# Attention over 32 sequences on one core: reciprocals of softmax sums formed on Pool, and gates from tanh

## The reference

```python
scores = jnp.einsum('bhqd,bhkd->bhqk', q, k) / jnp.sqrt(dk)      # layer 2: 16 heads of 8; layer 3: 16 heads of 64
attn = jax.nn.softmax(scores, axis=-1)
ctx = jnp.einsum('bhqk,bhkd->bhqd', attn, v)
...
# layer 2, slots (64 per batch entry), a GRU step on the routed inputs gi
r = jax.nn.sigmoid(xr + hr)
z = jax.nn.sigmoid(xz + hz)
n = jnp.tanh(xn + r * hn)
h_new = (1.0 - z) * n + z * hs
```

## Time and profile before

| what | value |
|---|---|
| time before, median of 3 runs | 2606.22 us (2602.77 to 2616.06) |
| time of the profiled execution | 2609.04 us |
| its span, first to last instruction | 2607.1 us |
| busy: PE, DVE, ACT, POOL | 78%, 59%, 51%, 24% of the span |
| mean granted TensorE clock | 0.872 of full speed |

### The profile page before, as it was taken

The page is one execution under the profiler, slowest core; times in us unless marked ns, Lnnn a source line. Parts: engine busy times, 40 slices in busy tenths (PEclk is TensorE's granted clock), DMA queues, the critical chain, the costliest instruction groups (busy, mean ns, idle before and its releaser), DMA issues.

```text
span 2607.1 us, 50762 instructions
## 1 busy us (share of the span) xinstructions
PE 2029.3 (78%) x17664; PEld 1624.5 (62%) x17666; DVE 1539.7 (59%) x4062; ACT 1316.8 (51%) x4486; POOL 629.4 (24%) x628
## 2 busy tenths in 40 slices
PE   3878888878788887345778888888888888788864
PEld 2667776767677765134556566666767666666654
DVE  5877676666576677633445565655556555554442
ACT  1755554545455655323456666555555555444411
POOL 0011112121211120012233342242332423222321
PEclk9789898899899988556589999998898989999987
DMA  7024443343444410300000011121212212222243
GB/s 227 26 77 123 125 135 92 121 128 106 117 140 124 131 53 1 129 30 20 12 9 12 5 53 57 57 72 57 72 59 64 60 58 72 59 87 70 80 141 100
DMA packets 149515, 205.94 MB, mean 79 GB/s; under 512 B 11088, under 2 KB 105360, under 8 KB 149008
## 3 DMA queue, kind: packets, MB, share of 16 engines
q1 hardware_dynamic: 141072, 185.90, 24.2%
q0 software_dynamic: 8192, 16.79, 2.1%
HBM read 162.80 MB, written 39.85 MB: 78 GB/s over the span
## 4 chain that ended last, share of the span: by engine, by line
PE 33%; DVE 9%; ACT 7%; issue 6%; POOL 1%; DMA 0%; DVEq 0%; ACTq 0%; SPq 0%; POOLq 0%
PE ps L1529 5%; PE ps L1752 5%; ACT pb L1915 4%; PE ps L1731 3%; DVE nm L2260 3%; PE ps L1562 3%; PE ps L1738 2%; ACT pt L1923 2%; PE ps L1589 2%; PE ps L1778 2%; PE ps L1571 2%; PE ps L1555 2%; DVE hT L2054 1%; PE ps L1770 1%; DVE hT L2049 1%
## 5 line engine op out<-in xcount | busy, mean ns | idle before, releaser
L1915 ACT ACTIVATE pb<-ps,nm 128x128 f32<-128x128 f32 x1024 | 363.2, 378 | 285.3 <-DVE nm L2260 276.3
L1956 POOL TENSOR_TENSOR pb<-pb,rcs 128x512 f32<-128x512 f32 x256 | 267.6, 1046 | 896.8 <-DVE rcs L2250 894.7
L936 ACT ACTIVATE pb<-pb,nm 128x128 f32<-128x128 f32 x1024 | 313.0, 392 | 88.1 <-DVE nm L1147 86.2
L2260 DVE TENSOR_REDUCE nm<-ps 128x8 f32<-128x1024 f32 x128 | 156.1, 1220 | 180.8 <-PE ps L1731 108.5
L1752 PE MATMUL ps<-w,pb 128*128 128x128 f32 x1024 | 177.6, 302 | 96.1 <-ACT pt L1923 74.1
L1915 ACT ACTIVATION_READ_ACCUMULATOR pb<-ps,nm 128x1 f32 x1024 | 223.0, 218 | 0.0
L2269 DVE COPY pt<-ps 128x512 f32<-128x512 f32 x128 | 88.3, 690 | 210.4 <-PE ps L1752 210.4
L1529 PE MATMUL ps<-hT,big 128*128 128x128 f32 x960 | 153.9, 310 | 72.7 <-DVE hT L2054 66.0
L1752 PEld LDWEIGHTS ps<-w,pb 128*128 128x128 f32 x1024 | 128.4, 155 | 129.1 <-issue 89.9
L1529 PEld LDWEIGHTS ps<-hT,big 128*128 128x128 f32 x960 | 135.3, 216 | 100.1 <-DVE hT L2054 79.9
L828 PE MATMUL ps<-w,pb 128*128 128x128 f32 x1024 | 160.0, 302 | 18.5 <-ACT pb L936 15.2
(11 more groups left out here) (355 smaller groups left out, 4457.2 us busy)
## 6 DMA issues: line engine op xcount, KB each, us to landing
big<-in_we SPq DMA_DIRECT2D x120, 514.0 KB
big<-in_we SPq DMA_DIRECT2D x120, 384.0 KB
big<-sorted_in SPq DMA_DIRECT2D x16, 960.0 KB
sorted_out<-big SPq DMA_DIRECT2D x32, 256.0 KB
sorted_in<-big SPq DMA_DIRECT2D x8, 960.0 KB, 9.0
hidden<-h_all SPq DMA_DIRECT2D x8, 512.0 KB, 2.9
h_all<-hidden SPq DMA_DIRECT2D x8, 512.0 KB, 3.9
sorted_out<-h_all SPq DMA_DIRECT2D x16, 256.0 KB
```

What stands on the lines that cost most here:

```text
L936: m = a.activation(pb[:, n % 2, k * S:(k + 1) * S], pb[:, n % 2, k * S:(k + 1) * S], ACT.Exp, bias=nm[:, n % 2, k:k + 1])
L1915: m = a.activation(pb[:, n % 2, e * S:(e + 1) * S], ps[:, half, k * S:(k + 1) * S], ACT.Exp, bias=nm[:, n % 2, e:e + 1], accum_out=sums[:, ...
L1956: g_.tensor_tensor(p4, p4, r4.unsqueeze(2).to_broadcast([P, 4, S]), ALU.mult).then_inc(n2["p_normed"], 1)
L2260: v.tensor_reduce(nm[:, n % 2, :], ps[:, 0:2, :].rearrange("p a (j k) -> p (a j) k", k=S), AX, ALU.max, negate=True).then_inc(n2["maxed"], 1)
```

## The change

The reciprocals of the sums leave DVE. In `norm`, POOL now waits for the exponentials itself, raises the four sums to the power -1 (a TENSOR_TENSOR with the new tile `minus`, 128 x 4), waits for that, and multiplies. `sums_inv` is gone from DVE's list, and so is its wait for `p_normed` two units before. The sigmoid of the gates is replaced by tanh(x/2): with t = tanh(x/2), sigmoid(x) is (t + 1)/2. The factor 1/2 of the first gate goes into `hn_c` in the setup (one more DVE instruction, once). The products with the gates become `scalar_tensor_tensor` with + 1 inside, and the factor 1/2 of the second gate goes into the last addition. The counts of instructions of the slots stay.

```diff
--- before.py
+++ after.py
@@ -129,6 +129,7 @@
         identb = sb("identb", [P, P], BF16)
         ones = sb("ones", [P, P])
         half = sb("half", [P, G])
+        minus = sb("minus", [P, 4])
         sc = sb("sc", [P, 16])
         hmax = sb("hmax", [P, NG * NC1])
         ymax = sb("ymax", [P, NG])
@@ -465,6 +466,7 @@
             def _(g):
                 g.memset(ones[:, :], 1.0)
                 g.memset(half[:, :], -0.5)
+                g.memset(minus[:, :], -1.0)
                 g.memset(hmax[:, :], 0.0)
                 g.memset(va[:, :, :, :], 0.0).then_inc(setup_g, 1)
                 g.wait_ge(setup_g, 1)
@@ -520,7 +522,8 @@
                 v.tensor_tensor(c1[0:HR, :], ps[0:HR, 3, 0:1], W("b1s", HR), ALU.add)
                 link(v.tensor_tensor(crz[:, :], ps[:, 4, 0:2 * D], R("bhh")[:, 0:2 * D], ALU.add))
                 v.tensor_tensor(crz[:, :], crz[:, :], R("bih")[:, 0:2 * D], ALU.add)
-                v.tensor_tensor(hn_c[:, :], ps[:, 4, 2 * D:3 * D], R("bhh")[:, 2 * D:3 * D], ALU.add)
+                link(v.tensor_tensor(hn_c[:, :], ps[:, 4, 2 * D:3 * D], R("bhh")[:, 2 * D:3 * D], ALU.add))
+                v.tensor_scalar(hn_c[:, :], hn_c[:, :], 0.5, None, ALU.mult)
 
             @block.tensor
             def _(pe):
@@ -1869,7 +1872,7 @@
                     g = group_at(hs, 22)
                     if g is not None and place == 2:
                         a.wait_ge(slot["rz_in"], g + 1)
-                        a.activation(rz, rz, ACT.Sigmoid).then_inc(slot["rz"], 1)
+                        a.activation(rz, rz, ACT.Tanh, scale=0.5).then_inc(slot["rz"], 1)
                     g = group_at(hs, 23)
                     if g is not None and place == 1:
                         a.wait_ge(slot["n_in"], g + 1)
@@ -1950,9 +1953,12 @@
                     g_.tensor_tensor(x_group(g), x_group(g), row_bcast(bias, G), ALU.add).then_inc(n2["bias_" + bias], 1)
 
                 def norm(n, half):
+                    g_.wait_ge(n2["exps"], 2 * n + half + 1)
+                    p4 = pb[:, n % 2, 4 * half * S:4 * (half + 1) * S].rearrange("p (k s) -> p k s", k=4)
+                    at = 8 * (n % 2) + 4 * half
+                    r4 = rcs[:, at:at + 4]
+                    g_.tensor_tensor(r4, sums[:, at:at + 4], minus[:, :], ALU.pow).then_inc(n2["sums_turned"], 1)
                     g_.wait_ge(n2["sums_turned"], 2 * n + half + 1)
-                    p4 = pb[:, n % 2, 4 * half * S:4 * (half + 1) * S].rearrange("p (k s) -> p k s", k=4)
-                    r4 = rcs[:, 8 * (n % 2) + 4 * half:8 * (n % 2) + 4 * half + 4]
                     g_.tensor_tensor(p4, p4, r4.unsqueeze(2).to_broadcast([P, 4, S]), ALU.mult).then_inc(n2["p_normed"], 1)
 
                 for hs in range(FIRST, LAST + 1):
@@ -2193,14 +2199,14 @@
                     if g is not None and place == 1:
                         v.wait_ge(slot["rz"], g + 1)
                         v.wait_ge(slot["xn_in"], g + 1)
-                        slink(v.tensor_tensor(rz[:, :, 0:D], rz[:, :, 0:D], hn_c[:, :].unsqueeze(1).to_broadcast(both),
-                                              ALU.mult))
+                        slink(v.scalar_tensor_tensor(rz[:, :, 0:D], rz[:, :, 0:D], 1.0,
+                                                     hn_c[:, :].unsqueeze(1).to_broadcast(both), ALU.add, ALU.mult))
                         v.tensor_tensor(xn, xn, rz[:, :, 0:D], ALU.add).then_inc(slot["n_in"], 1)
                     if g is not None and place == 2:
                         v.wait_ge(slot["n"], g + 1)
                         slink(v.tensor_tensor(hnew, hs_rows(), xn, ALU.subtract))
-                        slink(v.tensor_tensor(hnew, hnew, rz[:, :, D:2 * D], ALU.mult))
-                        v.tensor_tensor(hnew, hnew, xn, ALU.add).then_inc(slot["new"], 1)
+                        slink(v.scalar_tensor_tensor(hnew, rz[:, :, D:2 * D], 1.0, hnew, ALU.add, ALU.mult))
+                        v.scalar_tensor_tensor(hnew, hnew, 0.5, xn, ALU.mult, ALU.add).then_inc(slot["new"], 1)
                     g = group_at(hs, 24)
                     if g is not None and place == 2:
                         v.wait_ge(slot["val_psum"], g + 1)
@@ -2242,17 +2248,8 @@
                 def hs_rows():
                     return hs_c[:, :].unsqueeze(1).to_broadcast(both)
 
-                def sums_inv(n, half):
-                    at = 8 * (n % 2) + 4 * half
-                    v.wait_ge(n2["exps"], 2 * n + half + 1)
-                    if n >= 2:
-                        v.wait_ge(n2["p_normed"], 2 * (n - 2) + half + 1)
-                    v.reciprocal(rcs[:, at:at + 4], sums[:, at:at + 4]).then_inc(n2["sums_turned"], 1)
-
                 for hs in range(FIRST, LAST + 1):
                     n, p = unit_at.get(hs), unit_at.get(hs - 1)
-                    if p is not None:
-                        sums_inv(p, 1)
                     if n is not None:
                         v.wait_ge(n2["scores"], n + 1)
                         if n >= 2:
@@ -2260,8 +2257,6 @@
                         v.tensor_reduce(nm[:, n % 2, :], ps[:, 0:2, :].rearrange("p a (j k) -> p (a j) k", k=S), AX, ALU.max,
                                         negate=True).then_inc(n2["maxed"], 1)
                     work(1, hs)
-                    if n is not None:
-                        sums_inv(n, 0)
                     if p is not None:
                         v.wait_ge(n2["transposed"], 2 * p + 2)
                         if p >= 2:
```

## The result

The changed kernel takes 2633.64 us (median of 4 runs, 2629.57 to 2648.62) against 2606.33 us for the kernel before: a ratio of 1.011, 95% interval 1.0077 to 1.0143. It is slower, by more than the 0.5% that the measurement can tell, and outside my range of 2598 to 2628.

The account below looks back on a forecast made before the run. PE was busiest, 78% of 2607.1 us, with delays between engines costing full length in lone units. Terms +11.0 (way), -1.3 (DVE), -1.5 and -1.9 (gates) gave +6.3 us, so 2612.5 us, range 2598 to 2628.

Parts of the forecast that it names:

- The longer way (part 1): From exponentials to product on POOL, power and self-wait replace DVE's reciprocal and hop: 11.0 us slower, paid mainly in lone units.
- The first lone stage: Start of the second half, 1133 to 1315 us, where units do not overlap others: forecast 6 to 8 us longer.
- In the other units ... There the price is nothing: In at most 116 other units, every half is ready before PE transposes it, so the later product costs nothing.
- some 14 us lost to the products before: Estimate for the kernel before: DVE instructions lengthened by overlap with POOL's 256 wide products, some 14 us in all.
- rival 2: POOL's powers hold up DVE as its products do: 14 us lost again, half showing, 2620 us; chance 0.07 beyond +13.
- The sign that I had named: The forecast would be wrong if, among other signs, DVE's L2110 or L338 became longer.
- What DVE gets back: Of DVE's 43.9 us of reciprocals, only those directly ahead of something urgent count: 1.3 us faster.
- Part 2: Tanh for sigmoid at the gates: 16 table loads go, exponentials start 0.74 us earlier; 1.5 and 1.9 us gained.
- number 1: POOL becomes late more widely: all 32 lone units pay 1.1 us, 2636 us, half-way 2620 to 2628; chance 0.15 beyond +13.

Follow-up runs that it names:

- e4: Kernel before, plus an unused power on POOL ahead of its wait for DVE's reciprocal, which the product still uses: ratio 1.0030, again 1.0047.
- e2: Kernel before with the reciprocals as a power on POOL, the sigmoid left: ratio 1.0061, again 1.0083 and 1.0093.
- e9: Kernel before, plus one extra power of 128 x 4 on POOL behind each product, nobody waiting for it: ratio 1.0012.
- e5: No reciprocals on DVE or POOL; POOL multiplies by the sums directly behind the exponentials (results are no attention): ratio 1.0080 to the kernel before.
- e8: Kernel before, plus one extra product of constants, 128 x 384, on POOL behind each product, nobody waiting for it: ratio 1.0138.
- before_again: The kernel before, unchanged, run once more for a second profile: ratio 0.9977.

## Why the prediction was wrong

**The longer way (part 1): right.** Power 1.02 and self-wait 0.08 us forecast, 1.03 and 0.08 measured. The first lone stage 6 to 8 us longer forecast, 5.8, 6.1 and 4.9 in three profiles. The whole way 11.0 us forecast, 8 to 12 measured by e4, which has it nearly alone.

**"In the other units ... There the price is nothing": this step failed.** It asked whether each half of the probabilities is ready before PE transposes it. It is; but the product's place beside DVE moved, and that has a price of its own: held time rose from 16.4 to 48.7 us. The 25 to 27 us of it that e2 has above e4 went with 0.31 and 0.36%, 8 to 9 us, on two chips, and this is net of what DVE got back. I had the row in hand, `qm` up to 1309 ns beside wide work on POOL, and my estimate of some 14 us lost to the products before was near the 16.4. But I priced from it what powers might do (rival 2) and not what products would do when released earlier. The sign that I had named, a longer L2110, does not even show it (337 ns in the mean before, 340 after); the held time came in lines that the reciprocal had kept clear, the layer norms' L330 above all. The power is harmless (e9), and the product is not (e5, e8). The Trainium skill (GPSIMD Engine Reference, Key points) names contention in SBUF between GpSimd and those VectorE instructions that are in a two-port mode or have two SBUF inputs. The runs show it as 0.17 us becoming 1.00 for a wide product, and nothing for a power of four elements; which instructions are in a two-port mode no run here shows.

**"What DVE gets back": half of it.** I forecast -1.3 us and saw the reciprocals as cost only. In the trace DVE is 5.0 us busier without them. No run has the 1.3 us by themselves. The reciprocals' other effect, to hold the product back until DVE turned to PSUM, stood in no row by itself but in the order of rows: 223 of the 256 products start within 0.1 us of a reciprocal's end.

**Part 2: the mechanism right, its size off.** The 16 loads went. The timeline at the gate of the earlier trace rows, in the kernel after:

```profile
1385.46 1.22 DVE L2257 TENSOR_REDUCE nm<-ps 128x8 f32<-128x1024 f32 x1
1385.58 0.63 ACT L1875 ACTIVATE h_all<-h_all 128x512 f32<-128x512 f32 x1 [2.37 <-DVE h_all L2195]
...
1386.71 0.37 ACT L1918 ACTIVATE pb<-ps,nm 128x128 f32<-128x128 f32 x1 [0.50 <-DVE nm L2257]
```

The exponentials are 0.03 us behind the maxima where they had been 0.78 behind. Forecast -3.4 us; alone it measured 0.28 to 0.49%, 7 to 12 us (4 to 12 by the medians), and beside a late product none was seen.

**The sum.** Forecast: 11.0 for the way, -1.3 for DVE, -3.4 for the gates, +6.3 in all. Measured: 8 to 12 for the way, 8 to 9 for the held time less what DVE got back, nothing seen for the gates, 16 to 21 in all, against 20.7 to 27.3 from the three ratios of the whole (0.79 to 1.10%). The rest is within the intervals and is not assigned. Of the rivals none was it: number 1 gives a time near this one, but by waits that did not become wide (34 in place of 24, not all 64 halves of the lone units), and e5 is slower with hardly any way to pay.

The version to keep is e1, the tanh gates with the reciprocal left on DVE: below both kernels at 0.9951, 0.9959 and 0.9972 of the kernel before, the last with 1 inside its interval.

## What to carry to other kernels

When an operation is moved off an engine, look not only at who waits for it but at what it kept apart: a short instruction can be the release that puts a wide POOL product beside DVE work that reads PSUM. Before such a release is made earlier, list what DVE does in the next microsecond and price each element-wise instruction that reads SBUF alone at the product's whole length. The shortest test is to add a second such instruction with nobody waiting for it, once wide and once narrow.

## What the runs showed of the hardware

A wide POOL product (128 x 512, 1.04 us) can hold an overlapping DVE instruction until it ends, if that is a TENSOR_SCALAR, TENSOR_TENSOR or SCALAR_TENSOR_TENSOR that reads SBUF alone: 0.17 to 1.00 and 0.47 to 1.28 us in the timelines above. Reciprocals (0.18 us) and everything that reads PSUM went on beside it. A power of 128 x 4 needs nearly the same time on POOL and holds nothing.

TensorE's clock has places at which two runs of one kernel go either way: step 84 takes 13.7, 13.7 and 19.2 us in the three profiles of e1. What differs is the clock. At step 84 the kernel before has a stretch at the lower of the two levels; the same step of e1_again, with the same work for PE, has none. The window of the kernel before:

```profile
1784.00:1804.00 20.00, 16.16 (x79) 11.49 (x80) 8.84 (x30) 6.25 (x23) 2.08 (x2) 0.59 0.19 53
```

The same step in e1_again:

```profile
1780.00:1794.00 14.00, 9.28 (x82) 6.79 (x79) 8.45 (x30) 6.82 (x24) 2.08 (x2) 1.00 0.26 73
```

79 of PE's instructions take 16.16 us at a clock of 0.59 and 82 take 9.28 at 1.00, and from the maxima of this step to the next it is 19.4 against 13.7 us. Such stretches, of 13.7 or 17.1 us, stand at steps 84 and 116 before, at 100 alone in e1_gates_only and e9, at 116 alone in e1_again, at 84 and 116 in e1_third. At all three of 84, 100 and 116 they stand in each of the eight profiles with much held time (three of after, three of e2, e5, e8), and of the other twelve only in that of before_again. They are why one profile's stage can't carry a verdict of half a per cent here, and it takes many runs, or many profiles. That held time makes them likelier is thus what the profiles suggest; no run sets out to show it. What took the gates' gain stays open.
